# A sort of 200,000 edges on one core: the plan of all chunks made once, sums by TensorE, two sets of buffers, chunks of 1152 edges

## What is computed

```python
support = xn @ weight                                   # 6250 x 256
msgs = edge_weight[:, None] * support[dst]              # one row an edge
agg = segment_sum(msgs, src, 6250)                      # summed by source node
gnn = relu(agg + bias + xn)
```

## Time and profile before

| what | us |
|---|---|
| three runs | 3516.59, 3519.9, 3548.82 |
| their median | 3519.9 |
| span of the profiled execution, first to last instruction | 3152.9 |
| the profiled execution's own device time | not given beside its span |
| counting pass ends | 61 |
| first scatter starts | 90.5 |
| last scatter landed | 552.4 |

### The profile page before, as it was taken

The page is one execution under the profiler, slowest core; times in us unless marked ns, Lnnn a source line. Parts: engine busy times, 40 slices in busy tenths (PEclk is TensorE's granted clock), DMA queues, the critical chain, the costliest instruction groups (busy, mean ns, idle before and its releaser), DMA issues.

```text
span 3152.9 us, 38421 instructions
## 1 busy us (share of the span) xinstructions
PE 2454.8 (78%) x10265; PEld 1815.6 (58%) x10265; DVE 2036.5 (65%) x4689; ACT 1314.5 (42%) x2998; POOL 2177.9 (69%) x2105
## 2 busy tenths in 40 slices
PE   6788775677777788787787787786876865799997
PEld 3666554455454455455555554564554543688887
DVE  8999987555555665856757757657658546566522
ACT  4334321444444344444443444444443431455543
POOL 1666657777777777777777777777777774466653
PEclk9766665888887799899898898898988876799999
DMA  3111140644445345445445444554454347566552
GB/s 124 39 40 40 40 104 9 130 118 125 117 117 120 102 118 132 117 118 130 119 117 129 117 119 119 126 120 116 118 126 117 105 141 252 142 137 148 113 102 43
DMA packets 421977, 352.03 MB, mean 112 GB/s; under 512 B 254038, under 2 KB 363292, under 8 KB 421660
## 3 DMA queue, kind: packets, MB, share of 16 engines
q0 software_dynamic: 105664, 244.72, 29.1%
q1 hardware_dynamic: 307628, 97.06, 14.0%
q10 hardware_dynamic: 8496, 8.09, 0.8%
HBM read 284.10 MB, written 59.99 MB: 109 GB/s over the span
## 4 chain that ended last, share of the span: by engine, by line
PE 27%; POOL 24%; DVE 11%; issue 11%; DMA 9%; DVEq 1%; ACT 1%; SPq 0%; POOLq 0%; ACTq 0%
POOL rows L830 22%; PE ps L1036 7%; PE ps L1110 5%; DMA rows<-support,t_dst 5%; DVE R L1725 4%; PE ps L1226 3%; DMA out<-y_w,zt 3%; PE ps L1214 3%; PE ps L1102 2%; PE ps L1070 1%; PE ps L1082 1%; POOL out L872 1%; PE ps L1083 1%; DVE xnT L1785 1%; PE ps L1053 1%
## 5 line engine op out<-in xcount | busy, mean ns | idle before, releaser
L830 POOL DMA_INDIRECT rows<-support,t_dst x1624 | 1580.8, 973 | 495.0 <-issue 466.9
L1036 PE MATMUL ps<-rows,hot 128*128 128x256 f32 x3248 | 938.3, 438 | 392.4 <-DMA rows<-support,t_dst 254.6
L1725 DVE TENSOR_TENSOR R<-R,ps 128x256 f32 x1624 | 682.2, 420 | 693.5 <-PE ps L1036 484.7
L1036 PEld LDWEIGHTS ps<-rows,hot 128*128 128x128 f32 x3248 | 673.3, 218 | 637.3 <-DMA rows<-support,t_dst 351.2
L1381 ACT ACTIVATE hot<-is_low,t_w 128x128 f32<-128x128 bf16 x1624 | 690.6, 514 | 179.4 <-DVE is_low L1710 105.1
L804 POOL DMA_INDIRECT slots<-rec,st_pos x224 | 308.2, 1376 | 230.8 <-issue 84.0
L872 POOL DMA_INDIRECT out<-y_w,zt x105 | 165.8, 1579 | 169.9 <-DMA out<-y_w,zt 82.8
L977 PE MATMUL ps<-spread,piece 128*128 128x64 bf16 x1568 | 197.9, 302 | 58.8 <-DVE spread L1621 58.8
L977 PEld LDWEIGHTS ps<-spread,piece 128*128 128x128 bf16 x1568 | 190.8, 146 | 70.6 <-DVE spread L1621 34.8
L1226 PE MATMUL ps<-w_all,h_t 128*128 x840 | 196.8, 388 | 2.3 <-DVE y_w L2065 2.3
L1214 PE MATMUL ps<-zt_t,w_sel 128*128 128x256 f32 (+1 forms) x912 | 194.6, 367 | 2.1 <-ACT zt_t L1460 2.1
(11 more groups left out here) (295 smaller groups left out, 2950.9 us busy)
## 6 DMA issues: line engine op xcount, KB each, us to landing
rows<-support,t_dst POOLq DMA_INDIRECT x1624, 2.8
zt<-routed SPq DMA_DIRECT2D x48, 268.0 KB, 3.1
xa<-in_x SPq DMA_DIRECT2D x24, 512.0 KB
w_all<-in_L_ffn_W SPq DMA_DIRECT2D x16, 512.0 KB, 10.2
R<-zeros SPq DMA_DIRECT2D x1, 6400.0 KB, 28.9
xin<-in_x SPq DMA_DIRECT2D x12, 512.0 KB
support<-sup_sb ACTq DMA_DIRECT2D x12, 512.0 KB, 3.1
xf<-in_x SPq DMA_DIRECT2D x12, 512.0 KB
```

Of the source, the lines that this page charges most:

```text
L830: pool.indirect_dma_start(out=rows[h][:, j, :], out_offset=None, in_=support, in_offset=bass.IndirectOffsetOnAxis(ap=t_dst[a][:, col:col + ...
L1036: last = pe.matmul(ps[q][:, t * D:(t + 1) * D], lhsT=hot[o][:, q * 2 + t, :], rhs=rows[h][:, q * 2 + t, :], start=True, stop=True)
L1725: dve.tensor_tensor(out=there, in0=there, in1=ps[q][:, t * D:(t + 1) * D], op=ALU.add).then_inc(carried, 1)
```

## The change

- A batch has 9 columns for a chunk instead of 7: 1152 edges a chunk, 22 batches instead of 28, 176 scatters instead of 224. `KP` is 118 instead of 104. The flags of 5 batches are kept instead of 10.
- The counts of a chunk go as one row of one partition to `chunk`, a table with a partition for each of the 88 chunks of a stream's position (small DMAs of ACT's queue, one a batch). From it the begins of all runs and the leaps between their rows in `slots` are made once, by a dozen DVE instructions and two products; `locate` and `next_runs` are gone. Each batch's begins come back as one row by a small DMA of SP (`load_row`) and are added to the ranks by one more product; each batch's run rows are 8 products of one column (`owners`) over a comparison that DVE makes (`own`).
- The tree of additions over `marks` is done by TensorE (`tree`): 12 products of 288 columns with the identity, one of 72 and eight of 64 down to 8 columns, into 4 rows that DVE reduces from PSUM. `marks` has 49 rows.
- `piece` and `spread` exist twice, and so does `rank`. The ranks of batch q+2, the sums of q+1 and the sort of q-1 stand beside the positions of q.
- The nodes go in 17 groups of 3 blocks, one a batch in the first 17 batches, with two buffers for `xin`.
- The zeros go to `R` in two DMAs: blocks 15 to 49 in the middle of the sort, blocks 0 to 14 on SP's queue behind the first load of `slots`.
- The loops over batches are written out instead of hardware loops.

```diff
 TAILE = NE - P * EDGE_COLS
-JT = 7
...
-PAIRS = NQ // 2
-assert NQ == 2 * PAIRS and PAIRS == FULL + 2
+PER = CH // STREAMS
+NM = NQ * PER
+assert NM <= P
+XB = 3
...
-KEPT = 10
+KEPT = 5
+FIELDS = KEPT + 4
 RUN = 16
-KP = 104
...
+            def load_row(q):
+                if q == 0:
+                    sp.wait_ge(plan_done, 1)
...
+                sp.dma_start(row_f[q % 2][0:1, :, :].rearrange("a (i s) b -> a i s b", s=STREAMS),
+                             first_h[q * PER:(q + 1) * PER, :, 0, 0:NB]).then_inc(row_in, 16)
...
+            def zero_sums(lo, hi):
+                sp.dma_start(R[:, lo:hi, :].rearrange("p a d -> p (a d)").bitcast(BF16).rearrange("p (a w) -> p a w", w=D * 2),
+                             zeros[:, None, 0:D * 2].to_broadcast([P, hi - lo, D * 2])).then_inc(r_zero, 16)
...
+            for q in range(NQ):
+                load_row(q)
...
+                if q == KEPT + 4:
+                    sp.wait_ge(op_done, KEPT)
+                    sp.wait_ge(oh_read, NQ + KEPT)
+                    sp.wait_ge(z_ready, 1)
+                    zero_sums(UNDER, NB + 1)
...
+            for q in range(NQ):
+                pe.wait_ge(oh_done, q + 1)
+                if q >= 2:
...
+                    last = pe.matmul(ps[q % 2][0:1, 0:NB * CH], lhsT=ones_bf[:, 0:1], rhs=rows_of(flagged(q), j),
+                                     start=(j == 0), stop=(j == JT - 1))
+                last.then_inc(oh_read, 1)
...
+            def ranks(q):
+                if q >= 1:
+                    pe.wait_ge(ranked_, q)
+                if q >= 3:
+                    pe.wait_ge(idx_done, q - 2)
+                if q >= KEPT:
+                    pe.wait_ge(oh_done, NQ + q - KEPT + 1)
                 for j in range(JT):
-                    last = pe.matmul(ps[1][:, 0:NB * CH], lhsT=tri_bf[:, :], rhs=flat(q, k, j, kept), start=(j == 0), stop=(j == JT - 1))
-                last.then_inc(oh_read, 1)
...
+            def owners(q):
+                pe.wait_ge(owned_done, q + 1)
+                if q + 2 >= 1:
+                    pe.wait_ge(ranked_, min(q + 2, NQ))
...
+                for c in range(CH):
+                    last = pe.matmul(ps[1][0:KP, NB * CH + c:NB * CH + c + 1], lhsT=owned[q % 2][:, :, c],
+                                     rhs=leap_t[:, q, c:c + 1], start=True, stop=True)
+                last.then_inc(placed, 1)
...
+            def tree(q):
+                pe.wait_ge(marked, q + 1)
+                summed_rows = ps[0][:, 0:BATCH * RT].rearrange("p (j r c) -> p j r c", r=RT, c=CH)
+                def rows_from(r):
+                    return pe.matmul(ps[0][:, 0:BATCH * RT], lhsT=ident_h[:, :], rhs=marks[:, :, r:r + RT, :],
+                                     start=(r == 0), stop=(r == NB - 1 - RT))
+                rows_from(0)
+                pe.matmul(summed_rows[:, :, 0, :], lhsT=ident_h[:, :], rhs=marks[:, :, NB - 1, :], start=False, stop=False,
+                          skip_group_check=True)
+                for i in range(DUP):
+                    pe.matmul(summed_rows[:, i + 1:JT, 0, :], lhsT=ident_h[:, :], rhs=same[:, i:DUP, i, :],
+                              start=False, stop=False, skip_group_check=True)
+                for r in range(RT, NB - 1, RT):
+                    last = rows_from(r)
+                last.then_inc(added, 1)
...
+            def sort(q, half):
+                if half == 0:
                     pe.wait_ge(op_done, q + 1)
-                for c in range(halves[0] * (CH // 2), halves[-1] * (CH // 2) + CH // 2):
...
+                    o = c % (CH // 2) * (RUN * NF)
...
                     for j in range(JT):
-                        last = pe.matmul(ps[2 + half][:, o:o + RUN * NF], lhsT=piece[:, j, :, c], rhs=spread[:, j, :, :, c],
-                                         start=(j == 0), stop=(j == JT - 1))
-                    if c % (CH // 2) == CH // 2 - 1:
-                        last.then_inc(sorted_, 1)
...
+            def products(n):
+                pe.wait_ge(trc_done, n + 1)
+                for j in range(xblocks(n)):
+                    b = n * XB + j
+                    if b >= 2:
+                        pe.wait_ge(sup_read, b - 1)
+                    for c in range(KC):
+                        last = pe.matmul(ps[5 + b % 2][:, 0:D], lhsT=xnT1[:, c, j * P:(j + 1) * P], rhs=wg_sb[:, c, :],
+                                         start=(c == 0), stop=(c == KC - 1))
+                    last.then_inc(sup_done, 1)
...
+            for q in range(NQ):
+                if q:
+                    sort(q - 1, 0)
+                owners(q)
+                if q + 2 < NQ:
+                    ranks(q + 2)
+                if q + 1 < NQ:
+                    tree(q + 1)
+                if q < NX:
+                    products(q)
+                if q:
+                    sort(q - 1, 1)
+                if q + 1 < NX:
+                    turn(q + 1)
+            sort(NQ - 1, 0)
+            sort(NQ - 1, 1)
...
+                if q == 0:
+                    act.wait_ge(consts, 2)
+                act.wait_ge(tallied, q + 1)
+                act.dma_start(chunk[q * PER:(q + 1) * PER, :, 0:NB],
+                              stage[k][0:1, :, :].rearrange("a (i s) b -> a i s b", s=STREAMS)).then_inc(compacted[k], 16)
...
+            def name_places(q):
+                act.wait_ge(placed, q + 1)
+                if q >= 2:
                     for s in range(STREAMS):
-                        act.wait_ge(scattered[s], q * (16 * CH // STREAMS) - 16 * CH // STREAMS)
-                act.activation(st_pos[k][:, :], top_shift[k][:, :], ACT.Identity, bias=k16[:, 1:2]).then_inc(idx_done, 1)
-            def pack(q, k, more=True):
...
+            for q in range(NQ):
+                if q + 1 < NX:
+                    deviate(q + 1)
+                if q:
+                    pack(q - 1, 0)
+                if q + 2 < NQ:
+                    copy_ranks(q + 2)
+                name_places(q)
+                if q + 1 < NX:
+                    normalise(q + 1)
+                if q < NX:
+                    take(q)
+                if q:
+                    pack(q - 1, 1)
+                if q + 1 < NX:
+                    copy_turned(q + 1)
+            pack(NQ - 1, 0)
+            pack(NQ - 1, 1)
...
+            def own(q):
+                dve.tensor_tensor(out=owned[q % 2][:, :, :], in0=first_t[:, q, :][:, None, :].to_broadcast([P, KP, CH]),
+                                  in1=iota_k[:, :, :], op=ALU.is_le).then_inc(owned_done, 1)
+            def mark_ranks(q):
+                dve.wait_ge(ranked_, q + 1)
+                dve.tensor_tensor(out=marks[:, :, :, :], in0=flagged(q), in1=rank[q % 2][:, None, :, :].to_broadcast([P, JT, NB, CH]),
+                                  op=ALU.mult)
+            def mark_same(q):
+                b3 = bkt[:, q * BATCH:(q + 1) * BATCH].rearrange("p (j c) -> p j c", c=CH)
+                dve.tensor_tensor(out=same[:, :, :, :], in0=b3[:, 1:JT, None, :].to_broadcast([P, DUP, DUP, CH]),
+                                  in1=b3[:, None, 0:DUP, :].to_broadcast([P, DUP, DUP, CH]), op=ALU.is_equal).then_inc(marked, 1)
+            def position(q):
+                dve.wait_ge(added, q + 1)
+                return seq.later(dve.tensor_reduce(out=pos[:, :].rearrange("p (j c) -> p j c", c=CH),
+                                                   in_=ps[0][:, 0:BATCH * RT].rearrange("p (j r c) -> p j c r", r=RT, c=CH), axis=AX,
+                                                   op=ALU.add))
...
+            def spread_out(q, low_made):
+                k = q % 2
+                if q >= 2:
+                    dve.wait_ge(sorted_, (q - 1) * 2)
...
+                seq.later(dve.tensor_tensor(out=place[:, :, :, :], in0=low3.to_broadcast([P, JT, RUN, CH]),
+                                            in1=iota_r[:, None, :, :].to_broadcast([P, JT, RUN, CH]), op=ALU.is_equal))
...
+            for q in range(NQ):
+                own(q)
+                pos_made = position(q)
+                if KEPT <= q + 2 < NQ:
+                    flag(q + 2)
+                if q + 1 < NQ:
+                    mark_ranks(q + 1)
+                high_made = name_high(q, pos_made)
+                if q + 1 < NQ:
+                    mark_same(q + 1)
+                seq.settle(high_made)
+                low_made = name_low(q)
+                if q + 1 < NX:
+                    scale(q + 1)
+                spread_out(q, low_made)
```

More of the change, by code:

```diff
@@ L88 @@
 DUMP = 2048
-ZEROS = 400
+ZEROS = 512
+UNDER = 15
 assert KP * RUN <= DUMP
@@ L1014, in _ @@
-            pe.wait_ge(mixw_in, 16 * MIXW_DMAS)
-            ranks(0, 0, True)
-            turn(0, GB)
-            products(0, 0)
-            over_sort(pe, None, 0, pair)
+                        last = pe.matmul(ps[2 + half][:, o:o + RUN * NF], lhsT=piece[q % 2][:, j, :, c],
+                                         rhs=spread[q % 2][:, j, :, :, c], start=(j == 0), stop=(j == JT - 1))
```

(62 more changed lines are left out.)

586 lines of the change are left out of this document (230 added, 356 removed).

## The result

Four runs of the changed kernel have a median of 3570.0 us (3553.4 to 3582.9), beside 3518.4 us (3516.6 to 3548.8) for the kernel before on the same chip: a ratio of 1.0134, 95% interval 1.0102 to 1.0166. The medians are 51.6 us apart; 3479 was forecast. The profiled execution took 3573.0 us.

What follows compares the result with a forecast made beforehand. DVE seemed the bound, POOL nearly; after it PE and POOL. 97.4 + 319.6 + 88.5 + 5 - 4 + 2 = 508.5, 43.9 before 552.4; less 3 at the seam, 3519.9 - 40.9 = 3479 us, range 3430 to 3550.

Steps and rivals of the forecast that it cites:

- the cost of a scatter on POOL: On POOL, 118 descriptors instead of 104 might add up to 13% of 0.99 us, 1 us a batch; nothing was taken.
- T1 and T2: Time of a sort batch: 18.8 us for the first 17 batches, 17.7 for the last 5, together 408 us.
- start, seam and fill: Around the batches: first scatter at 97.4 us, 3 us at the seam to the gathers, 5 us for the zeros.
- The signs that the prediction named: Profile after: eight scatters in 17 to 20 us, DVE idle 3 to 5, PE busy over 90%, clock above 0.65.
- Its three signs of being wrong: In the sort: POOL keeps under 16 us a batch, the clock stays at 0.5, or POOL waits for `rec`.
- the forecast's sum for TensorE: TensorE's parts in a batch: 17.9 us at full clock, 24.7 at half; 18.7 taken with node work, 15 without.
- C: Rival: POOL held up little, PE at full clock; batches of 16.7, then 14.5 us; 3427 to 3458 us, chance 0.19.
- the walk through the held scatters: POOL under DVE's long instructions: 4 or 5 scatters in 13.2 us, the eighth ending at about 18 to 19.
- The time around the span: 367.0 us of the median 3519.9 were taken to lie around the span of 3152.9 and left as is.
- B: Rival: strided loads keep TensorE at half clock; first 17 batches 20 to 23.5 us each, time 3499 to 3559, chance 0.22.
- D: Rival: queues in lockstep once POOL waits over 4 us a batch for `rec`; batches about 24 us, time 3599, chance 0.12.
- A: The forecast: PE and POOL together bound the first 17 batches, 17.7 to 19.8 us each; 3460 to 3496 us, chance 0.47.

Runs made afterwards that it cites:

- The experiments on TensorE: Changed kernel with 120 rows, ratios to the kernel before: alone 0.9903, owners' weights padded to 128 columns 0.9904, row product read in order 0.9913.
- the two edits on TensorE: Changed kernel with 120 rows, owners' weights padded to 128 columns and row product reading in order, writing in strides: 3454.4 us, 0.9888 to the kernel before.

## Why the prediction was wrong

**The step that failed** is the one on the cost of a scatter on POOL: "118 descriptors instead of 104 may add up to 13% of the 0.99, 1 us a batch, or nothing; I take nothing". The bound of 13% took a scatter's time to grow with its rows. It grows with the rows of one engine, from 8 to 59, and measured 65%: 5.1 us for eight scatters. Each landing comes 1.7 us later behind the scatter's start, of which this is 0.65, and the longer waits for landings had no term. The prediction's own formula, with 22.8 us for T1 and T2, gives 3479 + 17 x 4.0 + 5 x 5.1 = 3573 us; 3570 was measured. So start, seam and fill hold, and the miss lies in T. Of the 92.8 us between the last landing forecast and measured (508.5 and 601.3), 72.7 go with 120 rows (528.6), which is this step; on one and the same chip 119 rows bring the last landing 74.9 us ahead of 118 (530.6 and 605.6). The other 20.1 us are put down to TensorE, below. The trace of before had one row count only, but the reason given for taking nothing, that the rows have no second size, was a reason for a range and not for zero.

The signs that the prediction named fail with it: eight scatters in 22.8 us instead of 17 to 20, DVE idle 10.7 us a batch instead of 3 to 5, TensorE busy 83% of the sort instead of over 90%, a clock of 0.63 instead of above 0.65. Its three signs of being wrong would not have told either: POOL kept over 16 us a batch, the clock was not 0.5, and POOL waited 0.7 us a batch for `rec`. None of them stood for a slower scatter.

**DVE** was right: 4.58, 2.56 and 1.99 us against 4.59, 2.55 and 1.99.

**TensorE**: 36 sort products in 4.6 us, right (4.56 and 4.55 at a clock of 0.50). With 120 rows the clock went as assumed: 0.50 through the ranks, 0.88 over the tree, and 1.00 from 315.7 to 318.2 us, in the products behind it. Owners 1.77 instead of 1.0 us: costed by the sort's products, whose weights have 128 columns where theirs have 118. The row product 1.05 instead of 0.19 to 0.36: costed by its columns, though it reads in strides from one partition. The strides are 0.3 us of it; why the rest, 0.76, is still above 0.36 stays open. Together up to 1.6 us a batch. These cost nothing while POOL is the bound; with 120 rows TensorE is, and the pace is 19.4 to 19.5 us, where the forecast's mean of 18.8 and 17.7 is 18.5. The experiments on TensorE add that even a right sum of parts isn't a right time: the tree took 1.51 or 2.80 us with nothing changed in it.

Two terms in the forecast's sum for TensorE are shown by no run. One is the 1.2 us by which 17.9 and 24.7 go down to 9.7 with 7.0 or 13.8, that is 16.7 (the T1 of C) or 23.5: it was the author's estimate. The kernel after showed this in its place: in the six steps of the timeline above from 343.46 to 359.99 us, the time of a group reaches 0.07 to 0.21 us past the start of the next, 0.99 together, and these ends are modelled. The other is what 17.9 and 24.7 hold for `products` and transposes, 3.5 and 6.9 us. Measured were twelve products in 2.75 us at a clock of 1.00 with 120 rows, and in 3.09 at 0.90 with the owners padded; in the kernel after, at 0.50, four products in 2.08 us and six transposes in 1.46.

**POOL**: the walk through the held scatters was right in its form (held to the end of `piece` and `spread`, then a fixed tail), and 0.65 us short in each. The one at 356.83 took 5.81 us beside a `tensor_tensor` of 4.58; what in a scatter waits for DVE, no run shows.

**Start and seam**: first scatter at 95.9 us against 97.4, inside its bounds. The seam took next to nothing: the gathers of the kernel after start at 605.37, 4.1 us behind the last landing, and soon go on at 1.25 us each. 3 us were set aside.

**The time around the span**: there is none. The kernel before run again has 1.7 us around its span, and the 367.0 us fit the difference of two chips in the gather stage. It did no harm, as the sort is alike on both.

**Rivals.** C (POOL held little) is out. B (half clock) is out too, though its T, 20 to 23.5 us, holds the 22.8 by luck: TensorE stood still for 86 of 501 us, and with 120 rows, where it is busy 355 of 361 us, its clock is 0.68 and not half. D has the right side and nearly the right time, 3599, with another trigger: it was to decide when POOL waits over 4 us a batch for `rec`, and POOL waits 0.7 (16.4 us in 22 batches). What came is its first half, `name_places` waiting for a landing (61.8 us in 14 waits from 110 to 471 us) with TensorE's products behind it (37.6 us), and slow scatters were what made the landings late. With 120 rows the same waits for `sup_sb` are 6.2 us. A, the forecast, is what the kernel with 120 rows does: last landing 528.6 against 508.5, and 28 us gained of 40.9.

The best version measured is the change with 120 rows, at 0.9903 and 0.9911. With the two edits on TensorE it had 0.9888 on another chip, whose interval holds both. Why 118 was taken can be guessed from the code: a chunk's runs are at most (1152 + 49 x 15) / 16 = 117.9, and 118 is that rounded up. Runs are whole, so 117 would do, which is 9 x 13; it wasn't tried.

**Left open**: the new plan with 117 rows and the kernel before with 112 weren't tried, nor another place for the tree in TensorE's order.

## What to carry to other kernels

Before a size goes into an indirect DMA, look at its divisors. Here the largest one up to 16 gave the shares: 118 rows went out as two of 59 (1.635 us a scatter on POOL) and 120 as fifteen of 8 (0.993 us), and these two rows of padding were worth some 2.2% of the kernel. When a trace has one size of an operation and the change makes another, the ratio of the sizes need not be the bound (13% more rows took 65% more here); find out what the operation is divided by. On a TensorE that was busy 355 of 361 us, 15.2 us taken out of one group did not come back, with a mean clock of 0.65 instead of 0.69; compare the groups behind it before counting the gain.

## What the runs showed of the hardware

- An indirect scatter occupies POOL for 0.944, 0.993, 1.083, 1.635 and 2.231 us with 112, 120, 119, 118 and 103 rows of the same size: 7, 8, 17, 59 and 103 rows for each engine, as the sizes of the packets show.
- A scatter under a DVE `tensor_tensor` ends a fixed time after it, 0.86 us with 8 rows for each engine and 1.51 with 59: the tail grows by the same 0.65 us as an unheld scatter.
- Eight products with one moving column each take 1.81 us with weights of 120 columns and 0.60 with 128, in fp16. A weight load takes 314 ns with 120 columns and 161 with 128 (110 to 471 us), and the mean of a product goes from 318 ns at 104 columns up to 347 at 120 and down to 196 at 128.
- A product over one partition with 392 columns takes 1.06 us when its moving operand is read in strides and 0.76 when in order, with the strides on the PSUM side.
- With one group shortened on a TensorE that is busy throughout, the mean granted clock was 0.65 instead of 0.69, and 15.2 us saved in one group were 15.9 us lost in others.
- On one chip the kernel before takes some 340 us more than on two others (3494 against 3154 and 3159 us). The profiles put such a difference into the idle time before the 1624 gathers, with the same busy time on POOL; its cause is open.
